# Diagonal quadrants for the inverse, split scores and an added tail for the attention: one transformer-like program on one core

## What is computed

```python
x = x + delta_rule(layernorm(x))     # 8 heads of 128, two keys and values for each token
x = x + ffn(layernorm(x))            # 256 -> 512 -> 512 -> 256, relu
x = x + attention(layernorm(x))      # 16 query heads, 4 key heads of 128, causal
x = x + ffn(layernorm(x))
```

```python
state = state * exp(g_t)
for j in range(2):
    corr = einsum('bhk,bhkv->bhv', k_t[:, j], state)
    u = (v_t[:, j] - corr) * b_t[:, j][..., None]
    state = state + einsum('bhk,bhv->bhkv', k_t[:, j], u)
o_t = einsum('bhk,bhkv->bhv', q_t, state)
```

```python
logits = einsum('bngqd,bnkd->bngqk', q, k) * scale + bias
logits = where(causal & (bias > 0), logits, finfo.min)
o = einsum('bngqk,bnkd->bngqd', softmax(logits), v)
```

## Time and profile before

| | |
|---|---|
| time, median of 3 runs | 4883.27 us (4879.52 to 4888.67) |
| the profiled execution | 4879.77 us, of which the trace spans 4878.0 |
| PE busy with products / with weight loads | 92% / 75% of the span |
| DVE / ACT / POOL busy | 59% / 45% / 24% |
| delta rule, units and attention, turns | 64 and 2, about 39 us each; 32, about 46 us each |

### The profile page before, as it was taken

How to read it: one execution, slowest core, us unless ns; L and a number is a source line. 1 busy time by engine, 2 the same in 40 slices (tenths; PEclk the granted TensorE clock), 3 DMA queues, 4 the chain that set the end, 5 groups by cost and what they waited for, 6 DMA issues and landing times. The chain is left out here.

```text
span 4878.0 us, 87441 instructions
## 1 busy us (share of the span) xinstructions
PE 4470.0 (92%) x27647; PEld 3678.8 (75%) x27647; DVE 2889.1 (59%) x7476; ACT 2192.6 (45%) x5668; POOL 1173.2 (24%) x2691
## 2 busy tenths in 40 slices
PE   3599999999999999999999689789999999999979
PEld 3488888888888888888888578656666666666668
DVE  5566666666666666666666345255555555555545
ACT  2344555555555455555555234244444444444434
POOL 5233443433433344434343000000000000000000
PEclk9999999999999999999999699799999999999989
DMA  7333333333333333333333232211111111111011
GB/s 265 129 93 95 98 91 100 92 96 114 96 100 91 95 100 91 100 91 92 106 106 93 70 105 78 73 43 47 34 43 34 47 43 34 47 43 29 23 58 35
DMA packets 558410, 392.49 MB, mean 80 GB/s; under 512 B 253040, under 2 KB 504944, under 8 KB 556400
## 3 DMA queue, kind: packets, MB, share of 16 engines
q1 hardware_dynamic: 557936, 386.69, 25.7%
HBM read 288.36 MB, written 98.14 MB: 79 GB/s over the span
## 5 line engine op out<-in xcount | busy, mean ns | idle before, releaser
L928 DVE SCALAR_TENSOR_TENSOR g_conv<-g_r,g_taps,g_conv 128x511 f32<-128x511 f32 (+2 forms) x961 | 702.9, 742 | 152.9 <-ACT g_conv L813 131.5
L817 ACT ACTIVATE g_us<-g_chn 128x128 f32<-128x128 f32 x528 | 146.1, 277 | 744.7 <-PE g_chn L629 743.8
L593 PE MATMUL g_lev<-g_nu,g_T 128*128 128x128 f32 (+1 forms) x3120 | 432.3, 279 | 0.8 <-DVE g_nu L940 0.8
L1954 ACT ACTIVATE a_pr<-a_pr,a_low 128x128 f32<-128x128 f32 (+3 forms) x512 | 286.9, 561 | 313.3 <-DVE a_low L2096 309.4
L593 PEld LDWEIGHTS g_lev<-g_nu,g_T 128*128 128x128 f32 (+1 forms) x3120 | 379.4, 177 | 33.5 <-issue 11.8
L1744 PE MATMUL a_sc<-a_kT,a_qT 128*128 128x128 f32 (+3 forms) x1024 | 340.3, 459 | 60.6 <-DVE a_low L2096 55.9
L1108 POOL TENSOR_TENSOR g_prod<-g_small 64x14 f32<-64x14 f32 (+6 forms) x896 | 227.0, 253 | 685.9 <-DMA g_small<-lower_d 620.7
L2227 POOL TENSOR_TENSOR a_bias<-a_kb,a_start 128x128 f32<-128x128 f32 (+2 forms) x96 | 56.5, 617 | 1380.1 <-DVE a_low L2096 938.3
L562 PE MATMUL g_r<-g_x_hi,g_w_hi 128*128 128x512 f32 x770 | 358.8, 466 | 7.2 <-issue 4.0
L2096 DVE CUSTOM_DVE_ANT_0 a_pr<-a_sc,a_bias 128x128 f32<-128x128 f32 (+3 forms) x512 | 244.5, 486 | 193.9 <-issue 187.9
L586 PE MATMUL g_lev<-g_U,g_L 128*128 128x128 f32 x2340 | 332.6, 278 | 0.0
(11 more groups left out here) (347 smaller groups left out, 11353.3 us busy)
## 6 DMA issues: line engine op xcount, KB each, us to landing
g_w_hi<-ws_d SPq DMA_DIRECT2D x65, 768.0 KB, 5.6
g_w_lo<-ws_d SPq DMA_DIRECT2D x65, 768.0 KB, 6.8
lower_d<-g_L SPq DMA_DIRECT2D x64, 512.0 KB, 3.2
g_T<-low_d SPq DMA_DIRECT2D x64, 512.0 KB, 4.1
g_U<-upp_d SPq DMA_DIRECT2D x64, 512.0 KB, 5.3
a_w<-w_groups SPq DMA_DIRECT2D x32, 640.0 KB, 4.6
oT_d<-g_oT SPq DMA_DIRECT2D x67, 256.0 KB, 5.1
f_oT<-oT_d SPq DMA_DIRECT2D x8, 2048.0 KB, 9.1
```

The source lines that it names most:

```text
L593: mm = M.matmul(lev[hf][0:rows, c, :].rearrange("p (j n) -> p j n", j=2), T[0:rows, hf * HC + c, 0:rows], nu[0:rows, hf * HC + c, :].unsqu ...
L928: ins = V.scalar_tensor_tensor(out=y[:, k:L], in0=x[:, 0:L - k], scalar=tap, in1=y[:, k:L], op0=ALU.mult, op1=ALU.add)
L1954: A(pr[g % 2][:, i, 0:width(i)], pr[g % 2][:, i, 0:width(i)], ACT.Exp, scale=-1.0, bias=low[g % 2][:, i:i + 1], accum_out=tot[g % 2][:, i: ...
```

## The change

It touches two stages.

**Delta rule.** At the first two levels the products are restricted to the two diagonal 64x64 quadrants (`QUADS`) and, of 64 columns, to the 32 that are masked in anyway (`seconds`). `lev_nu` makes for chunk 0 one product with full weights that moves 32 columns and then overwrites its upper half by one 64x64 product, and for the other three chunks two 64x64 products each, quadrant 0 and 1 in turn. `lev_un` makes one full product for chunk 0 and two 64x64 products for each of the others. All of them move 32 columns. `lev_mask` reads half the elements, `lev_add` becomes two instructions on 64 partitions each. At the last level the 64x64 products move the 64 columns that are used rather than 128. The table `levels` follows.

**Attention.** Queries and keys are split: ACT copies the rounded part, DVE subtracts it (`q_hi`, `q_lo`, `k_hi`, `k_lo`), and a score tile is three float32r products. A query or key thus passes ACT and then DVE before `pa` is free, where one engine copied it. `scores` is cut in two calls, tiles 0 and 1 ahead of the next query's products, 2 and 3 behind them. The two products of 3 rows at the end of `values` go. In their place POOL multiplies the identity by the flags (`dg`), PE multiplies ones by it (one float32r product of 384 columns that leaves the flags in all partitions), DVE multiplies this by the summed values, now transposed (`vtT`), into `tl`, and `head_out` moves from ACT to DVE and adds `tl` to the bank. `tail_rows` becomes twelve products that move 3 columns. The wait for the flags' way through DVE stands behind `key` and no longer ahead of it; in exchange `query(t, g=3)` now waits for a key that goes through two engines.

```diff
+        HCOL = C // 2
+        QUADS = (slice(0, C), slice(C, P))
+        def seconds(m, l):
+            return m.rearrange("p (n k) -> p n k", k=2 << l)[:, :, 1 << l:2 << l]
@@ lev_nu
+                    if li < NLV - 1:
+                        for r in QUADS[1:] if c == 0 else QUADS:
+                            k = slice(0, P) if c == 0 else r
+                            mm = M.matmul(lev[hf][k, c, 0:HCOL].rearrange("p (j n) -> p j n", n=1 << l), Lm[o][k, hf * HC + c, k],
+                                          seconds(U[o][k, hf * HC + c, r], l), start=True, stop=True)
+                        if c == 0:
+                            r = QUADS[0]
+                            mm = M.matmul(lev[hf][r, c, 0:HCOL].rearrange("p (j n) -> p j n", n=1 << l), Lm[o][r, hf * HC + c, r],
+                                          seconds(U[o][r, hf * HC + c, r], l), start=True, stop=True)
+                        continue
-                        mm = M.matmul(lev[hf][0:C, c, :], Lm[o][C:P, hf * HC + c, 0:C], U[o][C:P, hf * HC + c, :], start=True, stop=True)
+                        mm = M.matmul(lev[hf][0:C, c, C:P], Lm[o][C:P, hf * HC + c, 0:C], U[o][C:P, hf * HC + c, C:P], start=True, stop=True)
@@ lev_un
+                    if li < NLV - 1:
+                        for r in (slice(0, P),) if c == 0 else QUADS:
+                            mm = M.matmul(lev[hf][r, c, 0:HCOL], T[r, hf * HC + c, r], nu[r, hf * HC + c, 0:HCOL], start=True, stop=True)
+                        continue
+                    if li == NLV - 1 and c:
+                        mm = M.matmul(lev[hf][0:C, c, 0:C], T[0:C, hf * HC + c, 0:C], nu[0:C, hf * HC + c, :], start=True, stop=True)
+                        continue
@@ lev_add
+                if li < NLV - 1:
+                    for r in QUADS:
+                        to = blk(half(U[o], hf)[r, :, r], l, 1)
+                        ins = V.tensor_tensor(to, to, packed(lev[hf][r, :, 0:HCOL], l), ALU.add)
@@ attention, PE
+                    product(sc[i % 2][:, 0:width(i)], [(q_hi[g % 2][:, at], q_lo[g % 2][:, at], k_hi[tp_][:, 0:width(i)], k_lo[tp_][:, 0:width(i)])]).then_inc(s["sc"], 1)
@@ flag_rows
+                pe.wait_ge(s["dg"], t + 1)
+                M.matmul(pb[:, 0:TAIL * P], ones[:], dg[:].rearrange("p i n -> p (i n)"), start=True, stop=True).then_inc(s["ftr"], 1)
@@ values
-                M.matmul(out[:, 0:TAIL * P], vt_hi[:, at], frow[:], start=False, stop=False)
-                M.matmul(out[:, 0:TAIL * P], vt_lo[:, at], frow[:], start=False, stop=True).then_inc(s["pv"], 1)
@@ turn, PE
-                scores(t, 1, here)
+                scores(t, 1, here, (0, 1))
                 pe.wait_ge(s["qT"], G * t + 2)
                 query(t, here, bp, 2)
+                scores(t, 1, here, (2, 3))
...
                 flag_rows(t)
-                if n == 0 or more:
-                    pe.wait_ge(s["frow"], t + 1)
...
                     key(t + 1, there, nb)
+                if n and more:
+                    pe.wait_ge(s["frow"], t + 1)
@@ ACT
+            def query(t, g):
+                act.wait_ge(s["q"], G * t + g + 1)
+                A(q_hi[g % 2][:], pa[:], ACT.Copy).then_inc(s["q_hi"], 1)
@@ DVE
+                V.tensor_tensor(q_lo[g % 2][:], pa[:], q_hi[g % 2][:], ALU.subtract).then_inc(s["qT"], 1)
+            def key(t, tp_):
+                dve.wait_ge(s["k_hi"], t + 1)
+                V.tensor_tensor(k_lo[tp_][:], pa[:], k_hi[tp_][:], ALU.subtract).then_inc(s["kT"], 1)
+            def head_out(t, tp_, g):
+                dve.wait_ge(s["pv"], G * t + g + 1)
+                dve.wait_ge(s["frow"], t + 1)
+                V.tensor_tensor(oT[tp_][:, g, :], out[:], tl[tp_][:], ALU.add).then_inc(s["oT"], 1)
@@ POOL
+            def diagonals(t):
+                pool.wait_ge(s["fl"], t + 1)
+                Gp.tensor_tensor(dg[:], cc["ident"].unsqueeze(1).to_broadcast([P, TAIL, P]), fl[:].unsqueeze(2).to_broadcast([P, TAIL, P]),
+                                 ALU.mult).then_inc(s["dg"], 1)
```

More of the change, by code:

```diff
@@ L1969, in turn @@
                 nxt = more or n < HKV - 1
[L1970 removed]
+                exps(t, 1, (0, 1))
+                query(t, 2)
+                exps(t, 1, (2, 3))
                 evac(t, 0)
[L1972 to L1976 removed]
+                if nxt:
+                    key(t + 1, there)
+                if n == 1 and more:
                     columns(b + 1, 1 - bp, 0, pb)
@@ L2203, in _ @@
             gate_end(0)
+            key(0, 0)
             query(0, 0)
```

168 lines of the change are left out of this document (92 added, 76 removed).

## The result

The changed kernel takes 4620.07 us (median of 4 runs, 4617.02 to 4624.06), the kernel before 4885.12 us beside it. The ratio is 0.9459, with a 95% interval of 0.9443 to 0.9475: 265 us less, where 130 were forecast.

The account below looks back on a forecast made before the run. PE was taken to bound both stages: attention -207 us and delta rule +77 make -130, from 4879.8 to 4750, or 4753 us as median of runs. Its own range was 4700 to 4815; the eight-in-ten range 4605 to 4925.

Parts of the forecast that it names:

- the value of p: Delta rule, first two levels: spacing of 64x64 passes moving 32 columns, taken as 0.055 us, bounded by 0.11 and half of 0.055.
- a rival with a chance of 0.14: Delta rule: both quadrants load and multiply side by side, p near 0.028, stage gains 69 us, time 4607; chance 0.14.
- The formula: Delta rule's added time over 65 units, written as 65 x (128p - 5.9) us; 77 us more.
- covered by the wait for ACT: Delta rule, first level: 0.6 of two `lev_un` groups' added 0.66 us falls into PE's 0.63 us wait for ACT's update copy.
- The 0.34 us for a round trip between shapes: Delta rule: each group mixing full and 64x64 products pays 0.34 us for changing shape and back, before and after.
- `values`, without tails: Attention: dropping the 3-row products at a head's end saves 0.64 us for each of 128 heads, 82 us.
- flags: Attention: one product replaces the flags' transposes and their wait for DVE, saving 0.95 us in 31 turns, 29 us.
- scores: Attention: float32r products and the split order cut a head from 2.9 to 1.9 us, wait for DVE gone; 128 us saved.
- queries, output, other: Attention: new PE waits for key, flags and split weights cost 1 us a turn, 32 us back, bounds 0 and 96.
- Slow passes: Delta rule: instruction stream can't feed long runs of small passes, p between 0.07 and 0.11; 4958 us at 0.08; chance 0.16.
- The clock: Delta rule's level groups: PE falls to half clock, costing 110 to 220 us, time 4863 to 4973; chance 0.08.
- A poorer attention: Attention: the split keeps PE waiting 3 us in each turn, 64 us more stay, time 4817; chance 0.12.

Follow-up runs that it names:

- `rev`: Changed kernel with the second half of the last level's groups turned round, so the 64x64 products of both halves touch: 4605.92 us, ratio 0.9426.
- `full32`: Changed kernel with its first two levels at full shape, moving 64 columns in `lev_nu` and 32 in `lev_un`, mask in two instructions: 4711.89 us, ratio 0.9634.

## Why the prediction was wrong

**The step that failed is the value of p**, the spacing of a 64x64 pass when neighbours lie in different quadrants. I took 0.055 from single-quadrant transposes, and had 0.028 as the lower bound and as a rival. Measured is 0.058 within a quadrant, so the row was right, and 0.031 for two that alternate; over the 104 passes of the first two levels that is 2.5 us a unit, 160 us. No row before shows two quadrants at work, because a group of the last level or of the transposes uses one only. The choice between the bounds went by the nearest row; but what the nearest row showed, a single stream, was the very thing in question. The Trainium skill's TensorEngine Tiling (Array Packing), section Key Properties, says that different tiles can load and multiply in parallel. It stood in the prediction beside a rival with a chance of 0.14, and the runs with half of the products and with sorted quadrants show it to be so.

**The formula had one p for two things.** 104 of its 128 passes alternate (0.031), but the 24 of the last level stay in one quadrant (0.058), and there 0.055 was right. Put into the formula, p = 0.028 gives some -150 us and not the rival's -69, whose own sum leaves the last level at 0.055. With the terms as they were measured the stage closes:

| a unit | forecast | measured |
|---|---|---|
| four `lev_nu` groups, each from 0.89 | to 1.33, +1.8 | 0.82 + 0.10 = 0.92, +0.1 |
| four `lev_un` groups, each from 0.89 | to 1.22, +1.3 | 0.71 + 0.10 = 0.81, -0.3 |
| last level, 24 passes | -1.3 | 24 x (0.109 - 0.058), -1.2 |
| covered by the wait for ACT | -0.6 | 0 |
| new wait for `at` | 0 | +0.5 |
| sum, times 65 | +77 us | -0.9, -60 us (the stage: -65) |

The 0.10 in the first two lines is lost behind a group: the two passes of the full product that follows start 0.21 us apart (823.77 and 823.98) where 0.11 is usual. The two lines contain the pace. Beside it, the two full passes that now move 32 columns take 0.24 us with the change of shape behind them, not 0.32, which makes 0.6 us in eight groups. The cover at `chain_s` 6 could not show, since the groups became shorter; with sorted quadrants `chain_u` 6 comes 0.56 us later and `chain_s` 6 0.28, so it would have covered half and not nine tenths. DVE's part was forecast right: a mask is 0.13 us shorter, an add 0.15 longer. **The new wait is the second step that failed**: I went through what is late behind the longer groups and never asked it of the shorter last level. Of its 0.6 us ahead of the projection the wait takes 0.5. The rival's 4607 came near by luck in part: its mechanism is the one measured, but it counted the first two levels at +0.3 us a unit, where they gave -0.2, and had no wait for `at`, which cost 0.5; the two cancel.

**The 0.34 us for a round trip between shapes** held roughly: `rev` removes two of them in a unit, one of which the wait for `at` swallows, and the transposes at the unit's end come 0.24 us earlier; with `at` early it is 0.96 against 0.41 for `at` alone, 0.55 for the two.

**The attention**, -196 for -207, term by term, by the distances from one product's start to the next added up by function:

| | forecast | measured |
|---|---|---|
| `values`, without tails | -82 | 362.7 to 280.5, -82 |
| flags | -29 | 35.5 to 8.4, -27 |
| scores | -128 | 326.0 to 278.5, -48 |
| queries, output, other | +32 | -39 |

The sum hides two errors of opposite sign. A head's scores took 326.0 / 128 = 2.5 us before, not 2.9: the forecast was 2.25 for the products and 0.65 for the wait, and the wait is worth 0.3. They take 2.2 now, not 1.9, since the wait did not go:

```profile
PEld a_sc L1737 <- DVE a_low L2138: 35.2, 42, 3.4
```

That is 0.27 us a head as the weight loads show it (0.94 before) and 0.14 by the products. And the new waits that were to cost 32 us hardly exist; the key's way shows with

```profile
PE a_pa L1737 <- DVE a_k_lo L2126: 4.9, 6, 1.4
```

and nothing for the queries. Instead queries and key lost 19 us (288.3 to 269.4) and the output 15 (241.6 to 226.5). The split isn't the reason, for without it they take 253.0 and 226.5; leaving out the 3-row products alone takes 6 off the output and 3 off the queries. For the rest no run shows the cause. So the attention's forecast came true in its total by luck: two terms held, the scores gave 80 us less and the remainder 71 more.

**The rivals.** Slow passes: out, 0.031 and 0.058. The clock: not in this kernel (0.99 in the stage, as before), but real. Two variants of the same groups, one sorted and one with half of its products left out, set it off, at a cost of 158 and 74 us. A poorer attention: out.

## What to carry to other kernels

A product on half of the array's rows and columns costs 0.058 us a pass here against 0.112 for a full one, and nothing if its neighbour in the queue keeps another quadrant busy for longer. But a group pays 0.34 us for entering and leaving the shape: with one full product and six passes in one quadrant, as at the last level, it is just level with full shape (an estimate: 0.22 + 6 x 0.058 + 0.34 = 0.91 us against 0.89), and alternating quadrants the price ate nearly all of the gain: 8 groups a unit, some 10 us in 4620. Put groups of one shape side by side before making them smaller. And where PE is shortened by half a microsecond in front of a hand-over, look at what the other engine does just before it: moving one DVE and one ACT instruction brought 32 and 37 us, two to six times as much as the quadrants.

## What was unexpected of the hardware

- Leaving work out made the kernel slower. With half the small products gone and every group as long as before, the granted clock of the delta rule fell from 1.00 to 0.97 and the time rose by 61 us. With all products, but sorted by quadrant, it is 0.93 over the stage (0.99 changed). In the fall shown above PE was at the level groups of 64x64 products just before, without a wait longer than 0.4 us. Why these orders lose the clock and the alternating one keeps it, no run here tells.
- PE started the products of a second quadrant three passes ahead of their place in line, 0.14 us behind the first quadrant's first pass (the sorted group above).
- Starts can be out of order, the signal was not early. In the changed kernel the pass that carries a `lev_nu` group's signal belongs to quadrant 1, and in all 260 groups of the first two levels two passes of quadrant 0 start behind it (at 823.53, 823.56 and 823.62 above). Where DVE sits waiting for the signal, its mask starts 0.36 us behind the pass that carries it and 0.27 us behind the last one (medians of 135 waits); with half of the products left out, where the signal's pass is the last, it is 0.26.
- A product with 128 weight columns that moves 32 or 64 columns stands 0.112 us from the next, as with 128 (`full32`). With 64 weight columns in one quadrant it is 0.058 for 32 and 64 moving columns alike, and 0.109 for 128.
- Two quadrants write the same bank of PSUM at the same time, in different partitions, and pay nothing for it: in a `lev_nu` group they start 0.013 us apart, each lasts 0.22 us, and quadrant 0's passes stand 0.058 us apart with quadrant 1 beside them and without.
